# Causal attention: f32r products for the late score blocks, and a new order behind them

## The reference

```python
x = x + attn_a(layernorm(x), wq, wk, wv, wo)      # the change is in here
x = x + ffn(layernorm(x), w_gate, w_up, w_down)
x = x + attn_b(layernorm(x), ...)                 # gated linear attention
x = x + ffn(layernorm(x), w_gate, w_up, w_down)

def attn_a(x, wq, wk, wv, wo):                    # 8 batches, T=1024, M=256, 2 heads of 128
    q, k, v = (einsum('btm,mhd->bhtd', x, w) for w in (wq, wk, wv))
    q, k = frac_rope(q) * D_HEAD ** -0.5, frac_rope(k) * D_HEAD ** -0.5
    s = einsum('bhid,bhjd->bhij', q, k) - NEG * less(i, j)
    o = einsum('bhij,bhjd->bhid', softmax(s), v)
    return einsum('bhid,hdm->bim', o, wo)
```

## Time and profile before

| | |
|---|---|
| median of three runs | 1885.28 us |
| the profiled execution | 1885.07 us, its span 1883.3 us |
| TensorE busy | 1828.9 us, 97% of the span |
| VectorE, ScalarE, GpSimd busy | 1394.4, 880.3, 592.0 us |
| granted TensorE clock, mean | 0.995 |
| attention phase | to about 541 us of the span, 65.6 us for a batch inside |

### The profile page before, as it was taken

The page is one execution under the profiler, slowest core; times in us unless marked ns, Lnnn a source line. Parts: engine busy times, 40 slices in busy tenths (PEclk is TensorE's granted clock), DMA queues, the critical chain, the costliest instruction groups (busy, mean ns, idle before and its releaser), DMA issues.

```text
span 1883.3 us, 37415 instructions
## 1 busy us (share of the span) xinstructions
PE 1828.9 (97%) x12929; PEld 1529.6 (81%) x12929; DVE 1394.4 (74%) x2679; ACT 880.3 (47%) x1717; POOL 592.0 (31%) x542
## 2 busy tenths in 40 slices
PE   8999999999999999989999999999999999999998
PEld 7888888888888888877777777878787877888887
DVE  6566566556668888778777878787878788888885
ACT  6656656665654444443333333333333332444443
POOL 5313203211332222233433333434343334522211
PEclk9999999999999999999999999999999999999999
DMA  7100000000022122120000000000000001222332
GB/s 246 43 1 0 0 0 0 0 0 0 13 48 59 29 33 31 28 63 13 13 12 12 11 11 11 11 11 11 11 11 11 12 12 22 40 58 63 64 59 54
DMA packets 230631, 53.21 MB, mean 28 GB/s; under 512 B 209696, under 2 KB 228768, under 8 KB 230176
## 3 DMA queue, kind: packets, MB, share of 16 engines
q1 hardware_dynamic: 229296, 49.53, 13.0%
q10 hardware_dynamic: 1264, 2.76, 0.4%
HBM read 18.69 MB, written 8.39 MB: 14 GB/s over the span
## 4 chain that ended last, share of the span: by engine, by line
PE 70%; DVE 14%; issue 7%; POOL 4%; ACT 2%; SPq 1%; DMA 1%; DVEq 0%; ACTq 0%; POOLq 0%
PE PS L1212 16%; PE PS L1221 9%; PE PS L331 8%; PE PS L870 7%; PE PS L841 6%; PE PS L340 5%; PE PS L1750 3%; PE PS L859 3%; PE PS L1729 3%; PE PS L881 2%; PE PS L1679 2%; PE PS L1717 2%; DVE lin_zq L1515 2%; SPq L270 1%; PE PS L1740 1%
## 5 line engine op out<-in xcount | busy, mean ns | idle before, releaser
L331 PE MATMUL PS<-ln_xh,lin_w 128*128 128x512 f32 x768 | 249.9, 394 | 3.8 <-DVE lin_kT L1498 2.7
L1144 ACT ACTIVATE ff_silu<-PS 128x512 f32<-128x512 f32 x192 | 114.4, 597 | 235.5 <-PE PS L1212 207.3
L1179 DVE SCALAR_TENSOR_TENSOR ff_h<-PS,ff_silu 128x512 f32<-128x512 f32 x192 | 131.2, 684 | 113.1 <-PE PS L1212 99.3
L331 PEld LDWEIGHTS PS<-ln_xh,lin_w 128*128 128x128 f32 x768 | 145.2, 189 | 40.5 <-DVE lin_kT L1498 8.7
L577 POOL TENSOR_TENSOR qk<-qk,swapped 64x128 f32<-64x128 f32 (+2 forms) x96 | 96.9, 1010 | 240.1 <-DVE swapped L721 234.3
L1163 DVE TENSOR_TENSOR ff_h_lo<-ff_h,ff_h_hi 128x512 fp32r<-128x512 f32 x192 | 165.0, 860 | 0.4
L870 PE MATMUL PS<-probT,v_a 128*128 128x128 f32 x1152 | 153.3, 278 | 0.0
L870 PEld LDWEIGHTS PS<-probT,v_a 128*128 128x128 f32 x1152 | 139.5, 192 | 14.3 <-ACT probT L641 7.4
L331 PE MATMUL PS<-ln_xl,lin_w 128*128 128x512 f32 x384 | 150.7, 393 | 0.0
L841 PE MATMUL PS<-qk 128*128 128x512 f32 (+3 forms) x384 | 145.2, 489 | 0.9 <-POOL qk L577 0.9
L166 POOL TENSOR_SCALAR ln_var_eps<-ln_mean_var 128x4 f32<-128x4 f32 x64 | 15.5, 242 | 401.9 <-DVE ln_mean_var L139 401.9
(11 more groups left out here) (191 smaller groups left out, 5325.1 us busy)
## 6 DMA issues: line engine op xcount, KB each, us to landing
ff_raw<-ln_xn SPq DMA_DIRECT2D x464, 32.0 KB, 2.0
ln_xl<-ln_xn SPq DMA_DIRECT2D x288, 32.0 KB, 2.0
out_x<-X SPq DMA_DIRECT2D x15, 512.0 KB, 2.9
X<-in_x SPq DMA_DIRECT2D x7, 1024.0 KB, 5.4
stage<-in_w_lin SPq DMA_DIRECT2D x1, 2048.0 KB, 8.4
stage<-in_w_gate SPq DMA_DIRECT2D x2, 768.0 KB, 7.3
stage<-in_w_up SPq DMA_DIRECT2D x2, 768.0 KB, 8.7
stage<-in_w_down SPq DMA_DIRECT2D x2, 768.0 KB, 10.1
```

Source lines behind the costliest of these rows:

```text
L331: last = nc.tensor.matmul(out, w, x, start=n == 0, stop=n == len(terms) - 1)
L1144: nc.scalar.activation(silu[:, f % NB_GU, :], PS[:, f % NB_GU, :], ACT.Silu, scale=W_SCALE).then_inc(silu_done.sem, 1)
L1179: nc.vector.scalar_tensor_tensor(h[:, f % 2, :], PS[:, NB_GU + f % NB_GU, :], W_SCALE, silu[:, f % NB_GU, :], ALU.mult, ALU.mult).then_inc ...
```

## The change

From step n = 8 on (`LATE`), S(n) is made of three f32r products instead of one f32 product. For that k of both halves and q of the second half are split: ScalarE makes the high parts (`qk_high`, three copies of 128x1024, behind the probability evacuations of iterations 0, 1 and 3), GpSimd the low parts (three subtractions of 128x1024, behind the last rotation and ahead of the weight conversion of the first batch). S(8) waits for the last low part. The rotated q and k of half 1 now lie in `ln_xn`, so the normalisation of the next batch waits for the low parts too.

The order changes with it. On TensorE, S(n+2) with n+2 >= 8 moves from behind T(n) to behind O(n-2). On ScalarE, the exponential of n+1 moves behind `evacuate_out` in iterations 6 to 13, and behind the probability evacuation in 14. On VectorE, `out_low` goes ahead of `row_max` from iteration 5 on. The statistics go one token block to an iteration (1 to 8), the two aggregates to iterations 5 and 9, the normalisations to 10 and 12. In the last batch the following layer's normalisation moves from iteration 4 to 6, its transposition from 5 to 7, the second statistics from 7 to 8. The nine squares of the first batch go two at a time into iterations 12 to 15, the ninth last. The DMA scratch is set to 1024 bytes.

```diff
@@ -468,9 +468,14 @@
         sx = [SplitTransposed(nc, sems, f"a{half}", PS[:, 2 * half:2 * half + 2, :], ident, ln, half,
                               parts=env["norm"].parts if half == 0 else (sb("a1_xh", [P, KT, UN], F32R), sb("a1_xl", [P, KT, UN], F32R)))
               for half in range(NHALF)]
-        qk = sb("qk", [P, 2, HA, T])
-
-        wqkv_raw = qk[:].rearrange("p s h t -> p (s h t)")[:, 0:KT * (WQK + HA * DA)].rearrange("p (k n) -> p k n", k=KT)
+        LATE = HA * UT
+        qk_first = sb("qk", [P, 2, HA, UN])
+        k_hi, k_lo = sb("k_hi", [P, HA, T], F32R), sb("k_lo", [P, HA, T], F32R)
+        q_hi, q_lo = sb("q_hi", [P, HA, UN], F32R), sb("q_lo", [P, HA, UN], F32R)
+        qk = [qk_first[:],
+              env["norm"].xn[:].rearrange("p t m -> p (t m)").rearrange("p (s h t) -> p s h t", s=2, h=HA)]
+
+        wqkv_raw = qk_first[:].rearrange("p s h t -> p (s h t)")[:, 0:KT * (WQK + HA * DA)].rearrange("p (k n) -> p k n", k=KT)
         swapped = sb("swapped", [P, NHALF * 2, UN])
         V = sb("v_a", [P, TB, HA * DA])
 
...
@@ -516,6 +522,9 @@
             with eng.Fori(0, NB - 2) as p:
                 turn(p + 1, False, False)
             turn(NB - 1, False, True)
+
+        qk_parts = [(1, 0, k_hi[:, :, 0:UN], k_lo[:, :, 0:UN]), (0, 1, q_hi[:], q_lo[:]),
+                    (1, 1, k_hi[:, :, UN:T], k_lo[:, :, UN:T])]
 
         def score_rows(n):
 
...
@@ -573,10 +582,13 @@
                         for some in (slice(0, P), slice(P, UN)) if half == 0 else (slice(0, UN),):
                             for h in range(HA):
                                 rows = slice(h * ROT, (h + 1) * ROT)
-                                to = qk[rows, s, h, half * UN + some.start:half * UN + some.stop]
+                                to = qk[half][rows, s, h, some]
                                 done = nc.gpsimd.tensor_tensor(to, to, swapped[rows, 2 * half + s, some], ALU.add)
                             done.then_inc((first_rotated if some.stop == P else rotated).sem, 1)
                 pool.wait_ge(rotated.sem, rotated.at(b, 2 * NHALF))
+                for part, (s, half, hi, lo) in enumerate(qk_parts):
+                    pool.wait_ge(qk_hi_done.sem, qk_hi_done.at(b, part + 1))
+                    nc.gpsimd.tensor_tensor(lo, qk[half][:, s], hi.bitcast(F32), ALU.subtract).then_inc(qk_lo_done.sem, 1)
                 if first:
                     pool.wait_ge(env["ff_loaded"], 16 * NLOAD)
                     raw = env["stage"][:, 0:NW]
...
@@ -657,6 +669,11 @@
                     last = nc.scalar.activation(swapped[to:to + HALF, 2 * half + s, :], PS[of:of + HALF, PROJ_RING[m % 4], :], ACT.Copy)
                 last.then_inc(swap_done.sem, 1)
 
+            def qk_high(b, part):
+                s, half, hi, lo = qk_parts[part]
+                act.wait_ge(rotated.sem, rotated.at(b, 2 * half + s + 1))
+                nc.scalar.activation(hi, qk[half][:, s], ACT.Copy).then_inc(qk_hi_done.sem, 1)
+
             def square(part):
                 act.wait_ge(env["ff_low"], 1)
                 act.wait_ge(env["ff_squares"], part)
@@ -676,21 +693,29 @@
                 swap_halves(b, NPROJ - 1)
                 values(b, 1)
                 for n in range(NS):
-                    if n + 1 < NS:
+                    late = LATE <= n + 2 < NS
+                    if not late and n + 1 < LATE:
                         exp_step(b, n + 1)
                     evacuate_probs(b, n)
+                    if not late and n + 1 >= LATE and n + 1 < NS:
+                        exp_step(b, n + 1)
+                    if n in (0, 1, 3):
+                        qk_high(b, (n + 1) // 2)
                     if n == 0:
                         values(b, 2)
                     if n + 3 < TB:
                         values(b, n + 3)
+                    if n > 0:
+                        evacuate_out(b, n - 1)
+                    if late:
+                        exp_step(b, n + 1)
                     if n >= NS - NHALF and not last:
                         sx[n - (NS - NHALF)].act(act, b + 1)
                     if n == NS - 3 and last:
                         following.act_high(act, 0, 0)
-                    if n > 0:
-                        evacuate_out(b, n - 1)
-                    if first and n > NS - NPART:
-                        square(n - (NS - NPART) - 1)
+                    if first and n >= NS - NPART // 2:
+                        for part in range(2):
+                            square(2 * (n - (NS - NPART // 2)) + part)
                 if first:
                     square(NPART - 1)
                 evacuate_out(b, NS - 1)
@@ -711,7 +736,7 @@
                 half, s, h = m // NQK, m % NQK // HA, m % HA
                 at = slice(half * UN, (half + 1) * UN)
                 dve.wait_ge(proj_ready.sem, proj_ready.at(b, m + 1))
-                nc.vector.tensor_tensor(qk[:, s, h, at], PS[:, PROJ_RING[m % 4], :], cos[:, h, at],
+                nc.vector.tensor_tensor(qk[half][:, s, h, :], PS[:, PROJ_RING[m % 4], :], cos[:, h, at],
                                         ALU.mult).then_inc(cos_done.sem, 1)
 
             def times_sin(b, k):
@@ -765,25 +790,32 @@
                 times_sin(b, NPROJ // HA - 1)
                 for n in range(NS):
                     inverse(b, n)
+                    if n + 3 >= LATE:
+                        out_low(b, n - 1)
                     if n + 2 < NS:
                         row_max(b, n + 2)
                     elif not last:
                         sx[n + 2 - NS].dve(dve, b + 1)
-                    if n >= 1:
+                    if 1 <= n < LATE - 3:
                         out_low(b, n - 1)
                     if n >= 2:
                         residual(b, n - 2)
                     if not last:
-                        if n in (4, 6):
+                        if n == 1:
                             dve.wait_ge(x_loaded, (b + 1) * 16)
-                            ln.dve_stats(dve, b + 1, (n - 4) // 2)
-                        if n in (9, 11):
-                            ln.dve_normalise(dve, b + 1, (n - 9) // 2)
-                    if n == 4 and last:
+                        if 1 <= n <= TB:
+                            ln.dve_tile_stats(dve, b + 1, [n - 1])
+                        if n in (UT + 1, TB + 1):
+                            ln.dve_aggregate(dve, b + 1, n // TB)
+                        if n in (TB + 2, TB + 4):
+                            dve.wait_ge(qk_lo_done.sem, qk_lo_done.at(b, 3))
+                            ln.dve_normalise(dve, b + 1, (n - TB - 2) // 2)
+                    if n == 6 and last:
+                        dve.wait_ge(qk_lo_done.sem, qk_lo_done.at(b, 3))
                         following.ln.dve_normalise(dve, 0)
-                    if n == 5 and last:
+                    if n == 7 and last:
                         following.dve_blocks(dve, 0)
-                    if n == 7 and last:
+                    if n == 8 and last:
                         following.ln.dve_stats(dve, 1)
                     if n == 9 and last:
                         following.ln.dve_normalise(dve, 1)
@@ -831,15 +863,23 @@
                 i, h = steps[n]
                 if n == 0:
                     pe.wait_ge(first_rotated.sem, first_rotated.at(b, 2))
-                elif n == HA or n == HA * UT:
-                    pe.wait_ge(rotated.sem, rotated.at(b, 2 * (i // UT + 1)))
+                elif n == HA:
+                    pe.wait_ge(rotated.sem, rotated.at(b, 2))
+                elif n == LATE:
+                    pe.wait_ge(qk_lo_done.sem, qk_lo_done.at(b, 3))
                 keys = (i + 1) * P
                 for c in range(0, keys, UN):
                     w = min(UN, keys - c)
                     diag = c + w == keys
                     bank = PS[:, 2 * (n % 2) + c // UN, :]
-                    last = nc.tensor.matmul(bank[:, 0:w], qk[:, 0, h, i * P:(i + 1) * P], qk[:, 1, h, c:c + w],
-                                            start=True, stop=not diag)
+                    if n < LATE:
+                        last = nc.tensor.matmul(bank[:, 0:w], qk_first[:, 0, h, i * P:(i + 1) * P], qk_first[:, 1, h, c:c + w],
+                                                start=True, stop=not diag)
+                    else:
+                        q = slice(i * P - UN, (i + 1) * P - UN)
+                        for k, (q_part, k_part) in enumerate(((q_hi, k_hi), (q_hi, k_lo), (q_lo, k_hi))):
+                            last = nc.tensor.matmul(bank[:, 0:w], q_part[:, h, q], k_part[:, h, c:c + w],
+                                                    start=k == 0, stop=k == 2 and not diag)
                     if diag:
                         last = nc.tensor.matmul(bank[:, w - P:w], ident_b[:], mask_b[:], start=False, stop=True)
                 last.then_inc(s_ready.sem, 1)
@@ -914,9 +954,7 @@
                     if n < 2:
```

(12 more changed lines are left out.)

3 lines of the change are left out of this document (2 added, 1 removed).

## The result

The changed kernel takes 1900.97 us (1899.14 to 1903.51, 4 runs) against 1883.78 of the kernel before: ratio 1.0088, 95% interval 1.0068 to 1.0109. I had said 1880, with 1886 as the upper end. It is slower, and none of the reasons that I had listed came true.

A forecast was written before the change was run, and what follows sets the result against it. TensorE was taken to bound the attention's batch loop, busy 65.00 of 65 us; -9.8 (products) + 3.4 (waits) + 1.5 (first batch) + 0.6 (last) = -4.3 us gave 1880.8, stated as 1880, range 1872 to 1886.

The forecast's parts named there:

- The phases behind are untouched.: Phases after the attention's loop of batches: claimed not to be touched by the change, with no term in the sum.
- the products: Late scores on TensorE: three f32r products for one f32 save 1.22 us a batch, 9.8 us in the phase.
- the order: Early waits in each batch from the new order and copies: 0.42 us a batch, 3.4 us in all.
- The narrow f32r product: 128-wide piece of S at i = 4: three cost 0.21 to 0.65 us, upper end taken, making S 1.34.
- rival 1: Late scores: the narrow f32r matmul keeps its rate, giving 1874 to 1876 us; chance 0.35.
- The low part of W: W(5) in iteration 6 waits for the low part of W(4): 0.06 us once a batch.
- V(4): Early in each batch, V(4) waits for V(2)'s evacuation behind the first high copy: 0.36 us a batch.
- The exponential behind W: Iterations 6 to 13, ScalarE: the exponential fits before the next T by 0.03 to 0.2 us; cost 0.
- the low parts for S(8): GpSimd's three subtractions end at 172.9, S(8) due about 175.7: slack 2.8 us, cost 0.
- rivals 2 and 3: Rival 2: exponential behind W late, 1888 to 1893, chance 0.09; rival 3: low parts late for S(8), 1884, chance 0.05.
- The first batch: GpSimd's later conversions delay the normalisation and W(11): +1.5 us, or +0.2 if the overlap is free.
- The last batch: Next layer's steps moved into iterations 6 to 9 make VectorE late for W(9) and O: +0.6 us.

The follow-up runs named there:

- e1: Changed kernel plus 40 never-executed f32 matmuls ahead of the first feed-forward, moving the linear loop back onto 7 blocks: 1878.83 us, ratio 0.9973.
- e5: Changed kernel at e1's place, each late score one f32 product of the rounded high parts instead of three f32r products: 1892.8 us, ratio 1.0051.
- e7: e1 with VectorE's residual ahead of the row maximum in the iterations of the late scores: 1876.55 us, ratio 0.9960.
- e6: e1 with ScalarE's high copies behind the evacuations of the value blocks instead of ahead: 1881.59 us, ratio 0.9993.
- e9: e7 with the high copies one iteration later each and the last batch's block transposes in iteration 11 instead of 10: 1872.62 us, ratio 0.9937.
- e12: e1 with the next batch's layer-norm statistics and normalisation put back as in the kernel before, four tiles at once: 1887.88 us, ratio 1.0024.
- e10: Kernel before plus 15 never-executed f32 matmuls, the linear loop just ending inside its 7th block: 1884.61 us, one run.
- e11: Kernel before plus 17 never-executed f32 matmuls, the linear loop ending 7 instructions within an 8th block: 1905.17 us, one run.

## Why the prediction was wrong, step by step

**The step that failed** is the last sentence of the prediction's first paragraph: "The phases behind are untouched." That put the linear attention at nothing in the sum. Its lines are untouched, its place in TensorE's program is not, and that cost 22 us: 1900.97 us for the changed kernel, 1878.83 for the same kernel with the loop back on 7 blocks (e1). The trace of before had the sign of it. It fetches 12 instruction blocks from 840 to 1020 us and then one in all from 1000 to 1480, so the linear loop was living in the store, and a change that adds instructions ahead of it can end that. I counted matmuls by their time and never by their number. Neither the four rivals nor the range had room for 22 us.

**Without the place the forecast would have stood**: -5.1 us (e1) against -4.3 in the sum, and a batch of 64.74 to 64.76 us against 64.8. That is luck, since two terms were wrong by about as much in opposite directions: the products gave 1.78 us a batch where I had 1.22, and the order took 0.89 where I had 0.42.

- *The narrow f32r product.* The chain of the changed kernel, three S from iterations 6, 7 and 8 with the O ahead of each, answers the earlier trace rows:

```profile
238.20 0.61 PE PS L921 x3
238.81 0.98 PE PS L881 x6
...
241.20 0.60 PE PS L921 x3
241.79 0.98 PE PS L881 x6
...
244.29 0.49 PE PS L921 x3
244.78 1.04 PE PS L881 x6
```

  S of i = 4 costs 0.98 where I took 1.34; three narrow products are 0.98 - 0.69 = 0.29, 0.10 each. That is rival 1, between its two prices of 0.07 and 0.12, but the rate is not quite kept: 128 columns cost almost as much as the 0.12 of 256. In the timeline the weight loads of narrow products start 0.11 us apart (239.50 and 239.61 in e1), as those of the 256-wide ones do; whether they set the pace, no run shows. The sentence of the Trainium skill ("TensorE: Matmul & The Clock Gate", the part on fill) that the time goes by the columns would give 0.06, an estimate from 0.23 for 512; the measured 0.10 is nearer to that than to the 0.215 that I chose. The row of another data type was no bound on this side. S of i = 5, 6 and 7 came at 1.05, 1.21 and 1.39 as worked out. The term is 1.87 a batch from the chain and 1.78 from e5, not 1.22: mis-sized by some 0.6 a batch, 5 us.
- *O, which I had at 0.36 throughout.* It takes 0.61, 0.60, 0.49 and 0.40 in iterations 6 to 9, 0.66 us a batch more. Before, S(n+2) stood between T(n) and W(n-1). Now only T and W lie between S(n+1) and O(n-2), while the residual that frees O's single bank is queued behind the row maximum of that same S(n+1). These are the row maximum and the residual of VectorE's iteration 6 in e1. The residual ends at 241.27, and the O of iteration 7 starts at 241.32:

```profile
240.05 0.82 DVE L756 TENSOR_REDUCE neg_max<-PS 128x1 f32<-128x640 f32 x1 [0.91 <-PE PS L884]
240.79 0.48 DVE L769 SCALAR_TENSOR_TENSOR X<-PS,row_inv,X 128x256 f32 x1
```

  Iteration 6 is a case of its own, since S(7) was issued long before. There the maximum of S(7) stands behind `out_low`, for which VectorE stands idle 1.22 us, and the residual comes last of the three; no run shows this one apart. I had asked of every moved step what waits for it, and not of O, which stands where it stood and lost its cover. e7 shows the cause for iterations 7 to 9 and gives them back.
- *The low part of W.* I had a wait of 0.06 in iteration 6. W(5) takes 0.90 on the chain of e1 and 0.72 on that of before, so it was 0.18.
- *V(4).* From the end of T(1) to the end of V(4) the chain of e1 has 1.62 us, that of before 1.26: the 0.36 forecast, behind `v_a` L686. With O's 0.66 and W's 0.18 that is 1.20. The W's behind are some 0.05 shorter each in the new order (0.89 where before has 0.95, 1.12 where it has 1.17), which brings it near the 0.89 that e5 gives for the order. e6 and e9 show that it is the first copy: with e6 the wait moves to T, with e9 it goes. The chain of the changed kernel there:

```profile
225.28 0.39 ACT v_a L686
225.67 0.04 issue
225.71 0.98 PE PS L340 x6
```

- *The exponential behind W, the low parts for S(8).* There is no wait of T for `prob` and none of S for the low parts from 60 to 480 us: cost 0 was right, and rivals 2 and 3 did not come. The statistics belong to this. I had said that their block "held nobody", which is true of the old order; e12 shows that in the new one the block of 1.40 and 0.38 us stands ahead of `out_low` and holds W.
- *The first batch.* I had +1.5 for its waits. The first mark is 1.24 us earlier than before (1.03 in e1), where my steps give 0.7 later. The normalisation waits for `ln_rstd` as forecast (1.1 us, 1.3 said), but it then takes 1.38 us and not the 2.7 that I had for its overlap with the second 1/sigma. It is GpSimd's instruction that is longer, 1.23 us instead of 1.04. So W(11), for which I had a wait of 1.6, is late by some 0.3: on the chain of e1 it is 1.58 instead of 1.34, with 0.07 ahead of it. VectorE and then GpSimd of the changed kernel:

```profile
60.65 1.38 DVE L155 TENSOR_SCALAR ln_xn<-X,ln_mean_var,ln_rstd 128x256 f32<-128x256 f32 x4 [1.07 <-POOL ln_rstd L169]
```

```profile
60.84 1.23 POOL L169 TENSOR_TENSOR ln_rstd<-ln_var_eps,ln_minus_half 128x4 f32<-128x4 f32 x1
```

- *The last batch.* I had +0.6. W waits 2.25 us for `oT_lo` (2.15 in e1), because `dve_blocks` for the next layer waits on VectorE for a transfer, and `out_low` is queued behind it. "10 us to spare" was counted to the layer that uses the transfer, not to the instruction that waits for it. VectorE and then TensorE of the changed kernel:

```profile
518.20 1.25 DVE L255 STREAM_TRANSPOSE ln_xn<-ln_xn 128x1024 f32<-128x1024 f32 x1 [3.53 <-DMA ln_xl<-ln_xn]
519.37 0.12 DVE L761 RECIPROCAL row_inv<-row_sum 128x1 f32<-128x1 f32 x1
519.41 0.27 DVE L751 TENSOR_TENSOR oT_lo<-PS,oT_hi 128x128 fp32r<-128x128 f32 x1
```

```profile
519.82 2.90 PE L910 MATMUL PS<-probT,v_a 128*128 128x128 f32 x12 [2.25 <-DVE oT_lo L751]
```

  The wait has a second price in this execution. The granted clock is 0.50, the lower of its two levels, from 519.8 to 523.0, and the twelve matmuls take 2.90 us. In e1 they take 1.58, at a granted clock of 1.00, behind a wait of nearly the same length; in e7, behind 1.87 us, they take 2.70. From the seventh mark to the load of `lin_AD` before takes 353.6 us, the changed kernel 354.4 and e1 353.5, in which a batch's gain of 0.9 lies too: so the last batch lost some 1.7 and 0.9 us.

## What to carry to other kernels

Before you call a phase untouched, look at the DMA queue of instructions in its stretch. A loop that fetches nothing stays in the instruction store, and instructions added ahead of it, on the same engine, can push it over one more block. Here 96 instructions cost 22 us, and 163 more that are never executed gave them back. Count blocks touched, not instructions.

When a step is moved from between two others, ask of the one that stays what the gap had been hiding. And where a difference of one part in five hundred has to be seen, use a mark that repeats inside one execution beside the medians.

## What the hardware did that I had not expected

- A loop of 1645 instructions on TensorE runs without fetches while it touches 7 blocks of 256, and refetches some 9 blocks of 16.4 KB a turn once it touches 8: 8 instructions of displacement, 1884.6 to 1905.2 us (e10, e11, one run each). The direct stall is 2.1 to 2.6 us a turn. The turn is 3.2 to 4.3 us longer, and 5.7 and 6.3 in one turn each of the changed kernel and e11, in which the granted clock was 0.98.
- Three f32r matmuls of 128 columns take 0.29 us, 0.10 each. That is under half of the 0.22 of an f32 one of that width, but far more than a quarter of the 0.23 of 512 columns.
- Behind a wait of TensorE for `oT_lo` of 2.25 us (changed kernel), 1.87 (e7) and 3.48 (e12) the next twelve matmuls ran at about half speed, 2.90, 2.70 and 2.90 us; behind 2.15 us in e1 they did not (1.58).
- A VectorE normalisation of 1.38 us beside a 1/sigma on GpSimd kept its length, and GpSimd's instruction grew from 1.04 to 1.23 us. Beside a longer GpSimd subtraction the same normalisation had taken 3.54 us.
